# Cross attention of a fused decoder: more copies in flight early, every fifth key-block maximum copied by ScalarE, five pairs ahead of the loop instead of twelve

## The chip, the core and the metric

The kernel runs as one program on one core of a Trainium2 chip. The metric is the device time of one execution in microseconds (us); smaller is better.

## The reference

The program is a decoder of two layers on 1024 tokens of width 128, with a context of 6404 keys. Only the first cross attention concerns us here:

```
q = (x @ Wq + bq).reshape(1, 1024, 8, 16)      # 8 heads of 16
k = (ctx @ Wk + bk).reshape(1, 6404, 8, 16)
v = (ctx @ Wv + bv).reshape(1, 6404, 8, 16)
weight = softmax(einsum('bhqd,bhkd->bhqk', q, k) / 4)
out = einsum('bhqk,bhkd->bhqd', weight, v) @ Wo + bo
x = x + out
```

Before it stands a fast-weight attention, behind it a mixture of experts, a Mamba layer, a second cross attention and a second mixture. The change touches none of those.

## The kernel before

The stage is `xattn0_stage`. Its work is cut into four units: unit `u` is half of the tokens (512) for one group of four heads. Keys lie in SBUF as bf16 parts, features on the partitions. Softmax takes two passes over the keys. The first finds, for each query and head, the maximum score, from an approximate product of 64 rows. The second computes scores with the negative maximum as extra key and query rows, takes the exponential and weighs the values.

**First pass.** A pair is two heads of 128 queries against 496 keys: two matmuls side by side into two PSUM banks (`maximum`). A unit has 104 pairs, numbered so that four groups of 128 queries (`qt` 0 to 3) are innermost, then two head pairs (`h`), then 13 key blocks. VectorE reduces each bank (`take`, L1253). The ring for this is three banks, M0 to M2; entry `e` of the ring uses banks `2e % 3` and `(2e + 1) % 3`, so TensorE may fill entry `e` once the first bank of entry `e - 1` is free (`free_banks`, L1145).

**Early part.** The maxima of unit 0 come ahead of everything. Of each four pairs, three go into psE, are copied by ScalarE to `copied` in bf16 (L1101) and merged by VectorE into six running maxima (`merge`, L1266 and L1268). The fourth goes through the ring. There are 26 such groups of four. Then `end_running` folds the running maxima (L1275, L1278) and `give_maxima` turns 16 columns into three bf16 parts. TensorE transposes them (L1178), ScalarE copies them (L1083), and three transfers on SyncE's queue place them as rows of `qs` (L1055). The scores of unit 0 wait for these rows (`m_placed`).

**Lead.** Behind that, `LEAD` pairs of unit 1 go through the ring (one ahead of the transposition, the rest behind it) before TensorE comes to the first scores. Each has to have its banks freed by VectorE.

**Loop.** A unit has 51 tiles of 128 keys. For tile `t` TensorE issues, in this order: the scores of tile `t + 1` (two halves of two matmuls, L1158), then a pair of the next unit's first pass (call it *a*), then the weighing of tile `t` (`weigh`, L1171, eight records), then another pair (*c*). Some tiles have three pairs: the extra one stands between the halves of the scores, so the order is half, *a*, half, *b*, weigh, *c*. ScalarE takes the two exponentials of a tile (L1112); VectorE takes the pairs in turn. Once in a unit *c* is replaced by the transposition of the next unit's maxima (`PLACE_AT`), by the sums (L1183) and by the output projection (L1189). VectorE also inverts the sums in four pieces after the pairs of tiles 4, 8, 10 and 12 (L1316). The last pair of a unit is followed by `give_maxima` on VectorE.

SyncE issues the loads in program order on one queue: near keys (four blocks), queries of units 1 to 3, more constants, and then the far keys (heads 4 to 7, needed from unit 2 on), seven transfers of 832 KB and one of ones, also 832 KB. All that is issued by 420 us of the span. Behind it stand the rows of the maxima and the loads of the values.

Of the kernel before, what the change touches and what calls it, by code (L numbers as in the profile page):

```python
# [16 lines left out]
P = 128  # L17
# [5 lines left out]
BF16 = mybir.dt.bfloat16  # L23
# [3 lines left out]
ALU = mybir.AluOpType  # L27
ACT = mybir.ActivationFunctionType
# [920 lines left out]
def xattn0_stage(nc, k, d):  # L949
# [5 lines left out]
    with ExitStack() as ctx:  # L955
# [11 lines left out]
            .rearrange("p (i j n) -> p i j n", i=6, j=2)  # L967
        copied = sb("copied", [P, 2, 2, CHUNK0], BF16)
        maxima = sb("maxima", [P, 4, 4, CHUNKS0 + 1])
# [7 lines left out]
        psO = ps("O", [P, 512])  # L977
        psM = [ps(f"M{i}", [P, 512]) for i in range(3)]

# [6 lines left out]
        scored, exped, pv = sem("scored"), sem("exped"), sem("pv")  # L986
        max_mm, max_done = sem("max_mm"), sem("max_done")
        m_ready, m_tr, m_row, m_placed = sem("m_ready"), sem("m_tr"), sem("m_row"), sem("m_placed")
        o_copied, s_mm, s_copied, inverted, on_done, y_mm, y_done = [
            sem(n) for n in ("o_copied", "s_mm", "s_copied", "inverted", "on_done", "y_mm", "y_done")]  # L990
        LOADS = 2
        UNITS = 4
        PAIRS = 8 * CHUNKS0
        EARLY = PAIRS // 4
        LEAD = 12
        PLACE_AT, SUMS_AT, OUTPUT_AT = 46, 2, 20
        INVERT_AT = (4, 8, 10, 12)

        def kinds_in_tile(u, t):

            if u == UNITS - 1:
                return {SUMS_AT: ["sums"], OUTPUT_AT: ["output"]}.get(t, [])
            kinds = ["max"] * (3 if t in ((12, 24, 36) if u == 0 else (6, 14, 28, 36, 41)) else 2)
            if t == PLACE_AT:
                kinds[-1] = "place"
            if u and t == SUMS_AT:
                kinds[-1] = "sums"
            if u and t == OUTPUT_AT:
                kinds[-1] = "output"
            return kinds  # L1010
# [12 lines left out]
        def pair_place(pair):  # L1023

            return pair // 8, pair // 4 % 2, pair % 4

        with nc.Block() as block:
# [50 lines left out]
            def _(e):  # L1078
# [18 lines left out]
                for n in range(3 * EARLY):  # L1097
                    e.wait_ge(pre_mm, 2 * n + 2)
                    if n >= 2:
                        e.wait_ge(pre_merged, n - 1)  # L1100
                    nc.scalar.activation(copied[:, n % 2, :, :], psE[:, 2 * (n % 2):2 * (n % 2) + 2, 0:CHUNK0],  # L1101
                                         ACT.Copy).then_inc(pre_copied, 1)
                put_maxima_in_rows(0, EARLY + 1)

                def weights(u, t, g):
# [24 lines left out]
            def _(e):  # L1130
# [12 lines left out]
                def free_banks(entry):  # L1143

                    e.wait_ge(max_done, max(2 * entry - 1, 0))  # L1145
                    return psM[2 * entry % 3], psM[(2 * entry + 1) % 3]

                def next_maximum(u, pair, entry):
                    if (u, pair) == (2, 0):
                        e.wait_ge(far_keys_in, 16 * (len(K_ROWS) + 1))  # L1150
                    maximum(u, pair, [bank[:, 0:CHUNK0] for bank in free_banks(entry)], max_mm)

# [90 lines left out]
            def _(e):  # L1243
# [4 lines left out]
                def take(u, pair, entry):  # L1248
# [6 lines left out]
                    if pair == PAIRS - 1:  # L1255
                        e.wait_ge(max_done, 2 * entry + 2)
                        give_maxima(u)

                def merge(n, pair):
# [5 lines left out]
                    if n < 6:  # L1265
                        V.tensor_copy(mine, copied[:, n % 2, :, :]).then_inc(pre_merged, 1)  # L1266
                    else:
                        V.tensor_tensor(mine, mine, copied[:, n % 2, :, :], ALU.max).then_inc(pre_merged, 1)  # L1268

# [12 lines left out]
                def give_maxima(u):  # L1282
                    if u == 0:
                        end_running()
                    columns = maxima[:, :, :, 0:CHUNKS0 + (u == 0)]
                    step(V.tensor_reduce(mneg[:], columns.rearrange("p j q n -> p (j q) n"), AX.X, ALU.max, negate=True))
                    step(V.tensor_copy(mpart[:, 0, :], mneg[:]))
# [9 lines left out]
                def pass_on(semaphore, count, entry):  # L1297

                    e.wait_ge(semaphore, count)
                    if entry:  # L1300
                        e.wait_ge(max_done, 2 * entry)
                    e.sem_inc(max_done, 2)
# [25 lines left out]
                for u in range(UNITS):  # L1328
                    for t in range(TILES0):
                        for kind, entry, pair_unit, pair in in_tile.get((u, t), ()):  # L1330
                            if kind == "max":
                                take(pair_unit, pair, entry)
# [1614 lines left out]
```

## Time and profile before

| | us |
|---|---|
| median of 3 runs | 2831.26 (2829.81 to 2834.96) |
| profiled execution, its own time | 2832.58 |
| its span | 2830.8 |
| first pair of the early part starts | 386.1 |
| last reduction of the early part starts | 478.03 |
| first scores of the loop start | 501.09 |
| output of unit 0 copied | 640.36 |
| output of unit 3 copied | 1031.59 |
| stage over (last addition to x starts) | 1041.14 |

The span runs from the first to the last instruction; the execution's own time is 1.8 us more. Busy shares over the whole span are averages over six stages. In the table the stage lies between 386 and 1042 us. "Idle before" names the time for which an engine did nothing ahead of an instruction, and what ended it.

### The profile page before, as it was taken

How to read it: one execution, taken by the hardware profiler on the slowest of the kernel's cores; microseconds unless marked ns; L12 is line 12 of the kernel's file. 1: busy time of each engine (PE TensorE's matmuls, PEld its weight loads, DVE VectorE, ACT ScalarE, POOL GpSimd, SP SyncE). 2: the span in 40 equal slices, each digit the busy share in tenths (PEclk: the TensorE clock that was granted, in tenths of full speed). 3: DMA queues.
4: the chain of work that ended last, by engine and by line, in shares of the span. 5: the costliest groups of instructions: out<-in, count | busy, mean ns of one | idle time of the engine just before them, and what ended most of it. 6: DMA issues, size and time to landing. Idle time of an engine off the chain costs nothing. (4 is left out here: it accounts for less than half of the span.)

```text
span 2830.8 us, 35253 instructions
## 1 busy us (share of the span) xinstructions
PE 2419.0 (85%) x10344; PEld 891.7 (31%) x10344; DVE 2091.2 (74%) x3087; ACT 1538.3 (54%) x1858; POOL 297.4 (11%) x330
## 2 busy tenths in 40 slices
PE   5888735999999978999566589999999999995997
PEld 3655400222222123444222223333333333332443
DVE  5666648999998024444597889999999999966665
ACT  5544546676767962333343566666666666652111
POOL 4655600000000000000054000000000000000000
PEclk8998955999999989999688589999999999997998
DMA  4333399000000106766000521112003010112000
GB/s 115 131 125 122 130 150 113 21 24 25 24 25 25 32 27 180 191 191 182 24 0 12 116 78 45 30 55 77 29 29 103 29 30 29 32 35 103 0 0 7
DMA packets 186252, 190.66 MB, mean 67 GB/s; under 512 B 18464, under 2 KB 158181, under 8 KB 184801
## 3 DMA queue, kind: packets, MB, share of 16 engines
q1 hardware_dynamic: 186125, 189.00, 25.9%
q8 instruction: 75, 1.23, 0.2%
q14 instruction: 52, 0.43, 0.1%
HBM read 144.05 MB, written 41.42 MB: 66 GB/s over the span
## 5 line engine op out<-in xcount | busy, mean ns | idle before, releaser
L2468 DVE TENSOR_TENSOR y_acc<-y_acc,y_probs 128x1024 f32<-128x1024 f32 x408 | 496.2, 1216 | 33.8 <-ACT y_probs L2164 23.5
L2164 ACT ACTIVATE y_probs<-y_E,y_mask_bias 128x1024 f32<-128x1024 f32 x416 | 440.8, 1111 | 66.1 <-PE y_E L2249 66.0
L1112 ACT ACTIVATE x_probs<-x_E 128x1024 f32<-128x1024 f32 x408 | 396.8, 1021 | 137.0 <-PE x_E L1158 134.6
L1253 DVE TENSOR_REDUCE x_maxima<-x_M 128x1 f32<-128x496 f32 x676 | 420.1, 667 | 25.7 <-PE x_M L1140 14.0
L2258 PE MATMUL y_O<-y_probs,y_values 128*64 128x512 f32 x1664 | 402.3, 604 | 0.0
L2248 PE MATMUL y_E<-y_qa,y_ks 128*128 128x512 f16 x832 | 319.2, 384 | 1.2 <-ACT y_copied L2140 1.2
L2249 PE MATMUL y_E<-y_qb,y_ks 66*128 66x512 f16 x832 | 317.5, 382 | 0.0
L2140 ACT ACTIVATE y_copied<-y_M 128x1024 bf16<-128x1024 f32 x164 | 167.8, 1023 | 210.0 <-PE y_M L2215 210.0
L2406 DVE TENSOR_REDUCE y_maxima<-y_M 128x2 f32<-128x1024 f32 (+1 forms) x195 | 238.5, 1223 | 35.6 <-PE y_M L2215 23.5
L1577 DVE TENSOR_TENSOR f_hidden<-f_act_out,f_spread 128x512 f32<-128x512 f32 x160 | 110.6, 692 | 169.5 <-ACT f_act_out L1461 162.0
L1158 PE MATMUL x_E<-qs,x_keys 128*128 128x512 bf16 x816 | 220.2, 384 | 4.8 <-ACT x_probs L1112 2.9
L1171 PE MATMUL x_O<-x_probs,x_values 128*32 128x512 f32 x1632 | 217.3, 605 | 0.6 <-ACT x_probs L1112 0.6
L1461 ACT ACTIVATE f_act_out<-f_b 128x512 f32<-128x512 f32 x160 | 95.4, 597 | 185.0 <-PE f_b L1493 185.0
L2215 PE MATMUL y_M<-y_ks,y_qa 64*128 64x512 f16 x742 | 148.6, 397 | 26.8 <-DVE y_maxima L2406 24.1
L1498 PE MATMUL f_b<-f_hidden,f_weights 128*128 128x512 f32 x320 | 164.1, 596 | 4.9 <-DVE f_hidden L1577 4.9
L1493 PE MATMUL f_b<-f_xnT,f_weights 128*128 128x512 f32 x320 | 165.1, 598 | 1.1 <-ACT f_act_out L1461 1.1
L1140 PE MATMUL x_M<-x_keys,qs 64*128 64x496 bf16 x338 | 136.5, 404 | 23.8 <-DVE x_maxima L1253 23.3
L2258 PEld LDWEIGHTS y_O<-y_probs,y_values 128*64 128x64 f32 x1664 | 101.5, 136 | 171.1 <-issue 164.0
L2674 PE MATMUL g_b<-g_w_in,g_xT 128*128 128x512 f32 x256 | 120.0, 611 | 23.5 <-ACT g_xT L2634 17.0
L1140 PE MATMUL x_M<-x_keys,qm 64*128 64x496 bf16 x338 | 136.6, 404 | 0.0
L2417 DVE TENSOR_TENSOR y_running<-y_running,y_copied 128x1024 bf16<-128x1024 bf16 x192 | 131.1, 683 | 3.7 <-ACT y_copied L2140 3.4
L2248 PEld LDWEIGHTS y_E<-y_qa,y_ks 128*128 128x128 f16 x832 | 81.5, 98 | 141.5 <-issue 45.5
(460 smaller groups left out, 3035.7 us busy)
## 6 DMA issues: line engine op xcount, KB each, us to landing
f_spread<-comb_dram SPq DMA_DIRECT2D x160, 256.0 KB, 3.9
y_values<-v_dram SPq DMA_DIRECT2D x208, 128.0 KB, 2.2
v_dram<-a_v_out SPq DMA_DIRECT2D x26, 512.0 KB, 2.7
k_dram<-a_k_parts SPq DMA_DIRECT2D x26, 512.0 KB, 3.3
x_values<-v_dram SPq DMA_DIRECT2D x100, 128.0 KB, 2.1
f_weights<-f_w_in SPq DMA_DIRECT2D x80, 128.0 KB, 2.3
y_ks<-k_dram SPq DMA_DIRECT2D x75, 128.0 KB, 2.7
v_dram<-a_v_out SPq DMA_DIRECT2D x26, 256.0 KB, 2.0
```

What stands on the lines that cost most here:

```text
L1112: nc.scalar.activation(probs[:, n % 2, 2 * g:2 * g + 2, :], psE[:, 2 * g:2 * g + 2, :], ACT.Exp).then_inc(exped, 1)
L1140: T.matmul(banks[j], q, ks[r, 4 * (u // 2) + 2 * h + j, CHUNK0 * c:CHUNK0 * c + CHUNK0], start=True, stop=True).then_inc(done, 1)
L1158: ins = T.matmul(psE[:, j, :], ks[:, 4 * (u // 2) + j, P * t:P * t + P], qs[:, u, j, :], start=True, stop=True)
L1171: ins = T.matmul(psO[32 * j:32 * j + 32, :], values[:, i, 32 * j:32 * j + 32], probs[:, n % 2, j, :], start=(t == 0), stop=(t == TILES0 - ...
L1253: V.tensor_reduce(maxima[:, 2 * h + j, qt, c:c + 1], psM[(2 * entry + j) % 3][:, 0:CHUNK0], AX.X, ALU.max).then_inc(max_done, 1)
L2140: A(out, scores, ACT.Copy).then_inc(S["spare_copied"], 1)
L2164: A(probs[:, i, :], psE[:, 2 * (i % 2):2 * (i % 2) + 2, :].rearrange("p a b -> p (a b)"), ACT.Exp, bias=mask_bias[:, bass.ds(c * TILES_IN_ ...
L2248: T.matmul(psE[:, 2 * slot + j, :], ks1[:, u // 2 % 2, keys], qa[:, u, j, :], start=True, stop=False)
L2249: ins = T.matmul(psE[:, 2 * slot + j, :], ks2[:, u // 2 % 2, keys], qb[:, u, j, :], start=False, stop=True)
L2258: ins = T.matmul(psO[u % 2][DH1 * j:DH1 * j + DH1, :], values[:, i, DH1 * j:DH1 * j + DH1], probs[:, i, 512 * j:512 * j + 512], start=Fals ...
L2406: V.tensor_reduce(maxima[:, u % 2, :, 2 * g, bass.ds(c, 1)], psO_pair[:] if (u, g) == (0, 1) else psM[:], AX.X, ALU.max)\
L2468: ins = V.tensor_tensor(acc[:, u % 2, :], acc[:, u % 2, :], probs[:, i, :], ALU.add)
```

## The change

Four edits are made in `xattn0_stage`:

1. `copied` has four slots instead of two: in the early part, ScalarE's copy `n` waits for merge `n - 4` instead of `n - 2`.
2. In the loop, some *c* pairs (those with `qt` 2 or 3, at most every second tile, not the last eight pairs of a unit) are "spare": TensorE announces them on another semaphore, ScalarE copies both banks to bf16 after the second exponential of the next tile (`copy_spare`), in one instruction where the banks are neighbours, else in two. The first copy of each of four slots in a unit goes straight to `spares`; the others go to `copied` and are merged by VectorE two tiles later, ahead of its pairs (`merge_spare`). VectorE's reductions of these pairs are gone. The entry after a spare one needs ScalarE's whole copy. `give_maxima` first folds the four slots (`end_spares`) and afterwards resets `maxima`. By the selection loop 61 pairs of the loop are spare (21, 21 and 19 in the loops of units 0, 1 and 2), 20 of them copied in two pieces; 49 have a merge. (The loops hold 110, 104 and 93 pairs.)
3. `LEAD` is 5 instead of 12, and unit 0 has nine tiles of three pairs instead of three (110 pairs instead of 104; unit 2 has 93 instead of 92).
4. `PLACE_AT` is 47 instead of 46.

```diff
-        copied = sb("copied", [P, 2, 2, CHUNK0], BF16)
+        copied = sb("copied", [P, 4, 2, CHUNK0], BF16)
+        spares = sb("spares", [P, 4, 2, CHUNK0], BF16)
...
-        LEAD = 12
-        PLACE_AT, SUMS_AT, OUTPUT_AT = 46, 2, 20
+        LEAD = 5
+        PLACE_AT, SUMS_AT, OUTPUT_AT = 47, 2, 20
...
-            kinds = ["max"] * (3 if t in ((12, 24, 36) if u == 0 else (6, 14, 28, 36, 41)) else 2)
+            kinds = ["max"] * (3 if t in ((3, 8, 13, 18, 23, 28, 33, 38, 42) if u == 0 else (6, 14, 28, 36, 41)) else 2)
...
+        for u in range(UNITS - 1):
+            for t in range(TILES0 - 1):
+                kind, entry, unit, pair = in_tile.get((u, t), [("none", 0, 0, 0)])[-1]
+                _, h, qt = pair_place(pair)
+                if kind != "max" or qt < 2 or pair >= PAIRS - 8 or TILES0 * u + t < turn + 2:
+                    continue
+                slot, turn = 2 * h + qt - 2, TILES0 * u + t
+                new = (unit, slot) not in seen
+                seen.add((unit, slot))
+                spare[unit, pair] = len(spare), slot, None if new else merges
+                merges += not new
+                by_act.add(entry)
+                merge_at.setdefault(((turn + 2) // TILES0, (turn + 2) % TILES0), []).append((unit, pair))
...
                 for n in range(3 * EARLY):
                     e.wait_ge(pre_mm, 2 * n + 2)
-                    if n >= 2:
-                        e.wait_ge(pre_merged, n - 1)
+                    if n >= 4:
+                        e.wait_ge(pre_merged, n - 3)
...
+                def copy_spare(unit, pair, entry):
+                    n, slot, m = spare[unit, pair]
+                    e.wait_ge(spare_mm, 2 * n + 2)
+                    if m is None:
+                        if unit >= 2:
+                            e.wait_ge(m_ready, unit)
+                        out = spares[:, slot, :, :]
+                    else:
+                        if m >= 4:
+                            e.wait_ge(spare_merged, m - 3)
+                        out = copied[:, m % 4, :, :]
+                    bank = 2 * entry % 3
+                    if bank < 2:
+                        ins = nc.scalar.activation(out, psM3[:, bank:bank + 2, 0:CHUNK0], ACT.Copy)
+                    else:
+                        for j in range(2):
+                            ins = nc.scalar.activation(out[:, j, :], psM[(bank + j) % 3][:, 0:CHUNK0], ACT.Copy)
+                    ins.then_inc(spare_copied, 1)
...
                         weights(u, t, 1)
-                        for kind, entry, _, _ in in_tile.get((u, t - 1), ()):
+                        for kind, entry, pair_unit, pair in in_tile.get((u, t - 1), ()):
+                            if kind == "max" and (pair_unit, pair) in spare:
+                                copy_spare(pair_unit, pair, entry)
...
                 def free_banks(entry):
-                    e.wait_ge(max_done, max(2 * entry - 1, 0))
+                    if entry:
+                        e.wait_ge(max_done, vector_banks[entry - 1] + (entry - 1 not in by_act))
+                    if scalar_pairs[entry]:
+                        e.wait_ge(spare_copied, scalar_pairs[entry])
...
+                def end_spares(u):
+                    last = [found for (unit, _), found in spare.items() if unit <= u]
+                    e.wait_ge(spare_copied, len(last))
+                    e.wait_ge(spare_merged, sum(m is not None for _, _, m in last))
+                    width = CHUNK0
+                    while width > 62:
+                        width //= 2
+                        step(V.tensor_tensor(spares[:, :, :, 0:width], spares[:, :, :, 0:width],
+                                             spares[:, :, :, width:2 * width], ALU.max))
+                    for h in range(2):
+                        ins = V.tensor_reduce(maxima[:, 2 * h:2 * h + 2, 2:4, CHUNKS0].rearrange("p j q -> p q j"),
+                                              spares[:, 2 * h:2 * h + 2, :, 0:width], AX.X, ALU.max)
+                    step(ins)
...
                     if u == 0:
                         end_running()
+                    else:
+                        end_spares(u)
...
+                    if u + 1 < UNITS:
+                        step(V.memset(maxima[:], LOWEST))
...
                     for t in range(TILES0):
+                        for pair_unit, pair in merge_at.get((u, t), ()):
+                            merge_spare(pair_unit, pair)
```

`merge_spare` waits for the copy and the merge before, and issues one `V.tensor_tensor(mine, mine, copied[...], ALU.max)` on 128x992 bf16, the same form as L1268.

## Rows read from the trace of the kernel before

**Rows 1.** Windows of units 0 and 3: us busy (count) by engine, clock, DMA.
```profile
501.00:640.00 139.00, 135.82 (x825) 33.91 (x823) 130.80 (x216) 100.47 (x104) 0.00 (x0) 0.99 0.09 24
...
922.00:1031.00 109.00, 105.69 (x626) 21.02 (x618) 4.07 (x5) 98.79 (x103) 1.27 (x1) 1.00 0.11 31
```

**Rows 2.** Timeline of TensorE, one two-pair tile: start, length, instruction.
```profile
705.10 0.38 PE L1140 MATMUL x_M<-x_keys,qs 64*128 64x496 bf16 x1
...
706.41 0.38 PE L1140 MATMUL x_M<-x_keys,qs 64*128 64x496 bf16 x1
...
706.73 1.04 PE L1158 MATMUL x_E<-qs,x_keys 128*128 128x512 bf16 x4
...
707.70 0.38 PE L1140 MATMUL x_M<-x_keys,qs 64*128 64x496 bf16 x1
```

**Rows 3.** Reductions of one pair, in that tile's timeline, and their group.
```profile
L1253 DVE TENSOR_REDUCE x_maxima<-x_M x676: 608/665/676, 389.9 to 910.6; 128x1 f32<-128x496 f32 x169
...
705.52 1.25 DVE L1253 TENSOR_REDUCE x_maxima<-x_M 128x1 f32<-128x496 f32 x2
```

**Rows 4.** Timeline of TensorE around a tile of three pairs (unit 1, tile 6).
```profile
657.91 0.38 PE L1140 MATMUL x_M<-x_keys,qs 64*128 64x496 bf16 x1 [0.45 <-DVE x_maxima L1253]
...
659.06 0.38 PE L1140 MATMUL x_M<-x_keys,qs 64*128 64x496 bf16 x1 [0.23 <-DVE x_maxima L1253]
...
661.54 0.38 PE L1140 MATMUL x_M<-x_keys,qs 64*128 64x496 bf16 x1
```

**Rows 5.** The reciprocal ahead of that stall, in the timeline.
```profile
656.38 0.94 DVE L1316 RECIPROCAL x_recip<-x_sums 128x128 f32<-128x128 f32 x1
```

**Rows 6.** Timeline of ScalarE: two exponentials of a steady tile.
```profile
707.37 1.94 ACT L1112 ACTIVATE x_probs<-x_E 128x1024 f32<-128x1024 f32 x2 [0.66 <-PE x_E L1158]
```

**Rows 7.** ScalarE's early copies (timeline), and its copy of one bank.
```profile
398.43 2.79 ACT L1101 ACTIVATE x_copied<-x_E 128x992 bf16<-128x992 f32 x3 [0.75 <-PE x_E L1140]
...
L1089 ACT ACTIVATE x_o_sb<-x_O x4: 597/597/597, 640.4 to 1031.6; 128x512 f32<-128x512 f32 x4
```

**Rows 8.** VectorE's merges in one early group, timeline.
```profile
401.22 1.25 DVE L1268 TENSOR_TENSOR x_probs<-x_probs,x_copied 128x992 bf16<-128x992 bf16 x2
403.00 0.68 DVE L1268 TENSOR_TENSOR x_probs<-x_probs,x_copied 128x992 bf16<-128x992 bf16 x1 [0.54 <-ACT x_copied L1101]
```

**Rows 9.** TensorE's timeline, last lead pairs and first scores.
```profile
499.20 0.59 PE L1140 MATMUL x_M<-x_keys,qs 64*128 64x496 bf16 x1 [0.77 <-DVE x_maxima L1253]
...
500.56 0.59 PE L1140 MATMUL x_M<-x_keys,qs 64*128 64x496 bf16 x1 [0.76 <-DVE x_maxima L1253]
...
501.09 1.89 PE L1158 MATMUL x_E<-qs,x_keys 128*128 128x512 bf16 x4
...
504.69 0.38 PE L1140 MATMUL x_M<-x_keys,qs 64*128 64x496 bf16 x1
```

**Rows 10.** DMA issues from 375 to 500 us: size, median us to landing.
```profile
x_keys<-key_ones_in SPq DMA_DIRECT2D x1, 832.0 KB, 72.3
...
qs<-x_mrow SPq DMA_DIRECT2D x3, 4.0 KB, 3.7
```

**Rows 11.** Window with a low DMA share (last but one).
```profile
488.00:488.50 0.50, 0.18 (x2) 0.10 (x2) 0.50 (x2) 0.12 (x1) 0.00 (x0) 0.50 0.06 3
```

**Rows 12.** Timeline: VectorE's folding of the early maxima.
```profile
479.31 3.26 DVE L1275 TENSOR_TENSOR x_probs<-x_probs 128x2976 bf16<-128x2976 bf16 x3
482.60 0.99 DVE L1278 TENSOR_REDUCE x_maxima<-x_probs 128x6 f32<-128x372 bf16 x2
```

**Rows 13.** TensorE held by give_maxima in unit 0, timeline.
```profile
626.13 0.38 PE L1140 MATMUL x_M<-x_keys,qs 64*128 64x496 bf16 x1 [1.45 <-DVE x_maxima L1253]
```

**Rows 14.** Windows: granted clock behind the sums of unit 3, and at the first scores.
```profile
1036.00:1038.00 2.00, 0.00 (x0) 0.00 (x0) 1.63 (x3) 0.00 (x0) 0.29 (x1) 0.56 0.00 0
...
503.00:504.00 1.00, 0.76 (x2) 0.13 (x2) 0.00 (x0) 1.00 (x2) 0.00 (x0) 0.61 0.00 0
```

**Rows 15.** Timeline: the sums of unit 3.
```profile
1032.24 1.12 PE L1183 MATMUL x_M<-x_o_sb,x_sum_rows 128*128 128x512 f32 x2 [0.72 <-ACT x_o_sb L1089]
```

More of the change, by code:

```diff
@@ L977, in xattn0_stage @@
         psO = ps("O", [P, 512])
-        psM = [ps(f"M{i}", [P, 512]) for i in range(3)]
+        psM3 = ps("M", [P, 3, 512])
+        psM = [psM3[:, i, :] for i in range(3)]
         keys_in, far_keys_in = [sem(f"keys_in{b}") for b in range(4)], sem("far_keys_in")
@@ L987, in xattn0_stage @@
         max_mm, max_done = sem("max_mm"), sem("max_done")
+        spare_mm, spare_copied, spare_merged = sem("spare_mm"), sem("spare_copied"), sem("spare_merged")
         m_ready, m_tr, m_row, m_placed = sem("m_ready"), sem("m_tr"), sem("m_row"), sem("m_placed")
@@ L1025, in pair_place @@
             return pair // 8, pair // 4 % 2, pair % 4
+        spare, merge_at, by_act = {}, {}, set()
+        seen, merges, turn = set(), 0, -2
+        for u in range(UNITS - 1):
[11 more added lines that the diff above has]
+                merge_at.setdefault(((turn + 2) // TILES0, (turn + 2) % TILES0), []).append((unit, pair))
+        vector_banks = [2 * sum(e not in by_act for e in range(n)) for n in range(LAST_ENTRY + 3)]
+        scalar_pairs = [sum(e in by_act for e in range(n)) for n in range(LAST_ENTRY + 3)]
         with nc.Block() as block:
@@ L1098, in _ @@
                     e.wait_ge(pre_mm, 2 * n + 2)
-                    if n >= 2:
-                        e.wait_ge(pre_merged, n - 1)
-                    nc.scalar.activation(copied[:, n % 2, :, :], psE[:, 2 * (n % 2):2 * (n % 2) + 2, 0:CHUNK0],
+                    if n >= 4:
+                        e.wait_ge(pre_merged, n - 3)
+                    nc.scalar.activation(copied[:, n % 4, :, :], psE[:, 2 * (n % 2):2 * (n % 2) + 2, 0:CHUNK0],
                                          ACT.Copy).then_inc(pre_copied, 1)
@@ L1150, in next_maximum @@
                         e.wait_ge(far_keys_in, 16 * (len(K_ROWS) + 1))
-                    maximum(u, pair, [bank[:, 0:CHUNK0] for bank in free_banks(entry)], max_mm)
+                    maximum(u, pair, [bank[:, 0:CHUNK0] for bank in free_banks(entry)],
+                            spare_mm if (u, pair) in spare else max_mm)
                 def scores(u, t, g):
@@ L1255, in take @@
                     if pair == PAIRS - 1:
-                        e.wait_ge(max_done, 2 * entry + 2)
+                        e.wait_ge(max_done, vector_banks[entry] + 2)
                         give_maxima(u)
@@ L1265, in merge, with merge_spare @@
                     if n < 6:
-                        V.tensor_copy(mine, copied[:, n % 2, :, :]).then_inc(pre_merged, 1)
+                        V.tensor_copy(mine, copied[:, n % 4, :, :]).then_inc(pre_merged, 1)
                     else:
-                        V.tensor_tensor(mine, mine, copied[:, n % 2, :, :], ALU.max).then_inc(pre_merged, 1)
+                        V.tensor_tensor(mine, mine, copied[:, n % 4, :, :], ALU.max).then_inc(pre_merged, 1)
+                def merge_spare(unit, pair):
+                    n, slot, m = spare[unit, pair]
+                    if m is None:
+                        return
+                    e.wait_ge(spare_copied, n + 1)
+                    if m:
+                        e.wait_ge(spare_merged, m)
+                    mine = spares[:, slot, :, :]
+                    V.tensor_tensor(mine, mine, copied[:, m % 4, :, :], ALU.max).then_inc(spare_merged, 1)
+                def end_spares(u):
[11 more added lines that the diff above has]
+                    step(ins)
                 def end_running():
@@ L1284, in give_maxima @@
                         end_running()
-                    columns = maxima[:, :, :, 0:CHUNKS0 + (u == 0)]
-                    step(V.tensor_reduce(mneg[:], columns.rearrange("p j q n -> p (j q) n"), AX.X, ALU.max, negate=True))
+                    else:
+                        end_spares(u)
+                    step(V.tensor_reduce(mneg[:], maxima[:].rearrange("p j q n -> p (j q) n"), AX.X, ALU.max, negate=True))
+                    if u + 1 < UNITS:
+                        step(V.memset(maxima[:], LOWEST))
                     step(V.tensor_copy(mpart[:, 0, :], mneg[:]))
@@ L1300, in pass_on @@
                     if entry:
-                        e.wait_ge(max_done, 2 * entry)
+                        e.wait_ge(max_done, vector_banks[entry])
                     e.sem_inc(max_done, 2)
@@ L1329, in _ @@
                     for t in range(TILES0):
+                        for pair_unit, pair in merge_at.get((u, t), ()):
+                            merge_spare(pair_unit, pair)
                         for kind, entry, pair_unit, pair in in_tile.get((u, t), ()):
+                            if kind == "max" and (pair_unit, pair) in spare:
+                                continue
                             if kind == "max":
```

## The prediction

> **What bounds the kernel now.** I read the slices of the page first: all of the change lies in one stage, from 386 to 1042 us. Then I read windows by unit. In unit 0 TensorE is busy for 135.8 of 139 us at full clock, VectorE for 130.8, ScalarE for 100.5 [rows 1]. Two engines look full, and busy shares can't say which is the bound, so I read one tile in the timeline. The reader is to see that TensorE's starts leave nothing over: *a* to *c* 1.31 us (a pair and the weighing), *c* to scores 0.32, scores to the next *a* 0.97, in all 2.60 us a tile [rows 2], with no idle note on any of them. Taking a pair away from a tile would save some 0.31 us; having VectorE do less would save nothing.
>
> VectorE's records hide slack. Two reductions take 1.25 us of which one is 0.665, so the second starts 0.585 after the first [rows 3]. The first starts 0.42 after its matmul (705.10 to 705.52). VectorE is thus ready for the next pair 0.42 + 1.17 = 1.59 us after the matmul started, and that pair's reduction is wanted at 1.29 + 0.42 = 1.71: 0.12 us to spare. The bank for the next matmul is free at 0.42 + 0.665 + 0.06 = 1.15 us, wanted at 1.29: 0.14 us to spare. TensorE is the bound in two-pair tiles and VectorE follows closely, so any delay above about 0.26 us on VectorE is felt.
>
> It is felt in three places. In a three-pair tile the pairs follow at 1.15 us, not at the 0.8 that half the scores need; from the last pair of the tile before to the last of this one it takes 661.54 - 657.91 = 3.63 us, 1.04 more than a two-pair tile (2.59 to 2.60) [rows 4]. A reciprocal (0.86 us of VectorE's turn) leaves TensorE idle for 0.45 [rows 4, 5]. give_maxima leaves it idle for 1.45 [rows 13]. ScalarE waits 0.66 us in each tile for scores [rows 6]. In unit 3, with no pairs, a tile takes 109 / 51 = 2.14 us [rows 1].
>
> **Ahead of the loop.** In the early part ScalarE's third copy is late by one merge, which costs VectorE 0.54 us of idle time in a group [rows 8]; four slots take that away, 26 x 0.54 = 14 us. ScalarE's three copies need 2.79 us [rows 7], less than VectorE's five operations at about 0.59 (2.95), so nothing else steps in. The lead pairs are 1.36 us apart [rows 9]; seven fewer give 9.5 us. Together 23.5 us, if the loop could start then. It can't: it waits for the rows of the maxima, and these are transfers behind the far keys on one queue. The last of the far keys, issued at 419 us (see the order of issues), landed 72.3 us later, at 491.3; the rows issued from 486.85 on took 3.7 us although they are 4 KB each [rows 10]. The share of DMA fell only at 488 [rows 11]. No engine's work pulls that time forward. The rows would be issued near 473 now, and land when the backlog is gone, between 488 and 491.5. I take 490: the loop starts 501.1 - 490 = **11.1 us earlier** (9.6 to 13). Shortening the lead alone would give nearly all of it (501.1 - 9.5 = 491.6), so the 14 us of the early part are worth about 1.6.
>
> The Trainium skill (DMA: Bandwidth & Descriptors, section on queues, rings and completion order) says that each DMA engine takes the descriptors of one ring in order, while completion as a whole isn't in order of issue. The trace agrees with the first half: small transfers behind large ones land late, by the rows above. By the second half a small transfer on engines that drain early could land sooner; that is a rival below.
>
> **Moved pairs.** Seven pairs go from the lead into loops: six make three-pair tiles in unit 0 at 1.04 each [rows 4], one is an ordinary pair in unit 2 (0.31). **+6.5 us** (bounds 7 x 0.31 = 2.2, were VectorE no hindrance, and 7.3).
>
> **Waiting for ScalarE's copy.** A spare *c* started at, say, 706.41 is finished 0.38 later. ScalarE has just ended its second exponential (0.66 of idle time are next), so its copy starts at 0.42. It is a 128x992 copy; three take 2.79, and at about 0.9 between starts one takes 1.0 [rows 7]. Two halves take about 0.6 each, the second starting some 0.5 behind: 1.07. The next *a* needs the whole copy: 0.42 + 1.0 + 0.06 = 1.48 us after *c*, or 1.55, where it was wanted at 1.29. TensorE waits 0.19 us 41 times and 0.26 us 20 times: 13.0. VectorE would have freed a bank at 1.15, in time; so the copy is a new wait, on a shorter way. Before a three-pair tile (12 of them follow a spare *c*) the wait was there already, at 1.15, and becomes 1.48: 0.14 more than counted, 1.7. **+14.7 us** (bounds: 3, if a copy costs 0.05; 20, at 0.33 each).
>
> The exponentials are delayed by 0.42 + 0.9 - 0.96 = 0.36 us (0.43 in halves; scores are done at 0.32 + 0.64 = 0.96). TensorE needs the second one only for the second half of the scores of the next tile, 0.45 us after it ends now (707.37 - 0.66 = 706.71 against 706.73 + 0.43 = 707.16) [rows 2, 6]. So this is covered, barely; were it not, each spare pair would cost 0.36 to 0.43 instead of 0.19 to 0.26.
>
> **Merges.** A merge takes 0.585 us of VectorE's turn (1.25 - 0.665) [rows 8]. It stands right ahead of the reductions of *a*, two tiles after the copy. The hole that the missing reductions left was one tile earlier and is no use to it. By the reciprocal, 0.86 us gave a stall of 0.45 (the idle note; records overlap by up to 0.07, so 0.52) [rows 4, 5]: 0.34 to 0.41 is swallowed. With 0.34, estimated on the dear side, a merge costs 0.25; 49 of them 12.3. Where VectorE has no slack the full time counts: six fall into three-pair tiles by the selection (13, 28, 33 and 42 in unit 0, tile 6 in units 1 and 2), four follow a reciprocal (tiles 11 and 13 in units 1 and 2): 10 x 0.33 = 3.3. Two reciprocals, in tile 4 of units 1 and 2, stand where a spare pair is skipped and get hidden: -0.5 each. **+14.6 us** (bounds 8 at 0.17 each; 26 at the naive delay of 0.47).
>
> **Folding.** give_maxima now begins with end_spares: three maxima over 1984, 992 and 496 results. The early one had 2976, 1488 and 744 in 3.26 us [rows 12]; with 0.665 for 992 this is 0.13 fixed and 0.535 per thousand, so 2.35 us. Two reductions of 248 elements against two of 372 in 0.99 [rows 12]: 0.75. The memset of 224 elements has no row in this stage; I take 0.2, between nothing and 0.5 (one of those reductions). Sum 3.3 us, in which VectorE frees no bank. TensorE was idle already for 1.45 [rows 13], so all of it is felt in the loops of units 0 and 1. In unit 2 no pair follows; the transposition at tile 47 comes some 6.5 us after the last pair and would wait about 0.5. **+7.1 us** (6 to 8).
>
> **Clock.** TensorE would thus be idle for 1.45 + 3.3 = 4.75 us twice. After the sums of unit 3 it ended at 1033.4 [rows 15], and in the window from 1036 the granted clock is 0.56, so it fell from 2.4 to 1.2 GHz at about 1036.2, after 2.8 us without work [rows 14]. It should fall here too. At the loop's start, at 1.2 GHz, two rounds of scores and a start of *a* took 3.6 us for what is 2.3 at full clock [rows 2, 9]; the clock rose near 503.8 [rows 14]. **+2.6 us** for two falls (0 to 4).
>
> The Trainium skill (TensorE: Matmul & The Clock Gate, section on HAM oscillation) says that idle gaps between bursts of matmuls can throttle the clock anew each time. By it the sum keeps this term; with the clock held it would be 2863 us.
>
> **The sum.** -11.1 + 6.5 + 14.7 + 14.6 + 7.1 + 2.6 = **+34.4 us** against the profiled execution's own 2832.58, 1.3 above the median of 2831.26. From the median: **2866 us**. The bounds of the terms, not all on one side, give 2842 to 2884.
>
> **Rivals.**
> - *VectorE is the bound (faster).* Busy for 131 of 139 us [rows 1], it may hold TensorE all along in ways that no idle note shows. Then 12 spare pairs save 1.17 each and 49 save 0.585, 42.7 us, as far as TensorE allows. TensorE's own need in a unit is 51 x 1.97 (a tile without its two pairs) + 104 x 0.31 + about 2 = 135, against 139 in unit 0 and (922 - 640) / 2 = 141 in units 1 and 2: 18 us to gain at most. With -11.1, +2.2 for the pairs and +7.1 for the folding it gives -20: 2811. It decides if *a* comes within 1.29 us of a spare *c*. The idle notes in three-pair tiles speak for it, the evenness of rows 2 against. 0.10.
> - *ScalarE falls behind.* The exponentials' cover of 0.45 us isn't enough: 41 x 0.36 + 20 x 0.43 = 23.4 instead of 13.0. 2876. For it: 1.94 + 0.9 is more than a tile's 2.60 [rows 2, 6, 7]. Against: at most every second tile. 0.14.
> - *The rows overtake the far keys.* The loop starts when the lead is done, 23.5 us earlier instead of 11.1: 2854. Against: 3.7 us for 4 KB [rows 10]. 0.11.
> - *The new waits are nearly nothing* (0.05 for a copy, 0.17 for a merge, no fall of the clock): 2866 - 11 - 7 - 3 = 2845. 0.08.
>
> **The numbers.** My forecast has 0.54; 0.03 are left for a plain draw. Within 0.2% (5.7 us) is about what a measurement of this kernel can't tell from no change. Faster 0.12, same 0.06, slower 0.82. The range of 8 in 10 leaves out the faster rival and some of the tails: 2838 to 2882.
>
> **What would show it.** The first scores near 490 (near 478 if the rows overtake), after an idle wait that ends with the transfer to `qs`; early groups of about 2.95 us; *a* 1.48 us after a spare *c*, with ScalarE as releaser; *a* to *c* 1.5 to 1.6 in tiles with a merge; two idle times of about 4.8 us in units 0 and 1, and a clock below 1 behind them; units of 150 us or more. If unit 1 takes less than 138 us, TensorE wasn't the bound and I am wrong. If *a* follows a spare *c* in 1.3 us, the third term falls.

## The result and the profile after

The changed kernel takes 2883.06 us (median of 4, 2882.01 to 2887.2) where the kernel before took 2832.11 us beside it (2829.81 to 2834.96): a ratio of 1.0182, 95% interval 1.0164 to 1.0200, or 51 us more. The forecast was 2866 us, slower, with a range from 2838 to 2882. The direction was right; the size was two thirds of the real one, and the time lies 1 us above the range.

In the kernel after, L1101 has become L1122, L1158 is L1205, L1171 is L1218, the pairs (L1140) are L1183, their reductions (L1253) L1300, the early merges (L1268) L1315, the merges in the loop L1325, and ScalarE's copies of spare pairs L1150 (in one piece) and L1153 (in two).

First the way to the loop: timelines of VectorE, TensorE and SyncE of the kernel after, between 457 and 502 us.

```profile
457.43 1.25 DVE L1300 TENSOR_REDUCE x_maxima<-x_M 128x1 f32<-128x496 f32 x2
458.59 1.83 DVE L1315 TENSOR_TENSOR x_probs<-x_probs,x_copied 128x992 bf16<-128x992 bf16 x3
460.35 1.25 DVE L1300 TENSOR_REDUCE x_maxima<-x_M 128x1 f32<-128x496 f32 x2
...
476.64 0.59 PE L1183 MATMUL x_M<-x_keys,qs 64*128 64x496 bf16 x1 [0.77 <-DVE x_maxima L1300]
...
496.68 1.49 PE L1205 MATMUL x_E<-qs,x_keys 128*128 128x512 bf16 x3 [19.44 <-DMA qs<-x_mrow]
...
472.45 2.18 SPq L1076 DMA_DIRECT2D qs<-x_mrow  x3
```

An early group now takes 460.35 - 457.43 = 2.92 us, its three merges without a gap ([rows 8] had 0.54 us of idle time ahead of the third). The lead is done at 477. Then TensorE is idle for 19.4 us, and what ends that is a transfer. The same stretch in the view of DMA issues, and one window (DMA share last but one):

```profile
x_keys<-key_ones_in SPq DMA_DIRECT2D x1, 832.0 KB, 76.0
...
qs<-x_mrow SPq DMA_DIRECT2D x3, 4.0 KB, 22.2
...
490.00:492.00 2.00, 0.00 (x0) 0.00 (x0) 0.00 (x0) 0.00 (x0) 0.00 (x0) 0.50 0.99 107
```

Rows of 4 KB took 22.2 us to land where they took 3.7 in [rows 10]; the last transfer of the far keys, issued at 419.6, landed 76.0 later, at 495.6, and the queue is still full at 490 to 492. The loop starts at 496.7, 4.4 us earlier than the 501.1 of [rows 9].

Then the loop. Timeline of TensorE, ScalarE and VectorE of the kernel after, in unit 1 (tile 15, which has a merge ahead of *a* and a spare *c*, and the start of tile 16):

```profile
710.53 0.38 PE L1183 MATMUL x_M<-x_keys,qs 64*128 64x496 bf16 x1
...
712.14 0.38 PE L1183 MATMUL x_M<-x_keys,qs 64*128 64x496 bf16 x1 [0.23 <-DVE x_maxima L1300]
...
713.73 0.37 PE L1183 MATMUL x_M<-x_keys,qs 64*128 64x496 bf16 x1 [0.24 <-ACT x_copied L1150]
...
712.59 1.00 ACT L1150 ACTIVATE x_copied<-x_M 128x992 bf16<-128x992 f32 x1 [0.45 <-PE x_M L1183]
...
710.83 0.67 DVE L1325 TENSOR_TENSOR x_spares<-x_spares,x_copied 128x992 bf16<-128x992 bf16 x1
711.41 1.25 DVE L1300 TENSOR_REDUCE x_maxima<-x_M 128x1 f32<-128x496 f32 x2
```

The reader is to see two stretched steps. From *a* (710.53) to the spare *c* (712.14) it is 1.61 us instead of 1.31, since a merge stands ahead of the reductions of *a*. From that *c* to the next *a* (713.73) it is 1.59 instead of 1.29 [rows 2], since ScalarE's copy begins 0.45 after *c*, lasts 1.00, and TensorE starts another 0.14 behind its end. Both new waits are on TensorE's way.

Third, the folding: timelines of the kernel after at the end of unit 0, and windows with the granted clock (third from the right).

```profile
639.51 2.35 DVE L1334 TENSOR_TENSOR x_spares<-x_spares 128x1984 bf16<-128x1984 bf16 x3
641.90 0.73 DVE L1337 TENSOR_REDUCE x_maxima<-x_spares 128x4 f32<-128x248 bf16 x2
...
643.16 0.24 DVE L1360 MEMSET x_maxima<- 128x224 f32 x1
...
645.45 0.59 PE L1183 MATMUL x_M<-x_keys,qs 64*128 64x496 bf16 x1 [4.98 <-DVE x_maxima L1300]
...
644.00:648.00 4.00, 2.55 (x8) 0.64 (x8) 3.09 (x8) 0.95 (x2) 0.00 (x0) 0.58 0.02 4
...
651.00:652.00 1.00, 1.00 (x4) 0.25 (x2) 0.00 (x0) 1.00 (x2) 0.00 (x0) 0.78 0.00 0
```

TensorE's idle time is 4.98 us where [rows 13] have 1.45, and the clock behind it is 1.2 GHz until about 651.4. The end of unit 1 shows the same: 4.98 us of idle time until 806.89, and 1.2 GHz until about 811.9.

The waits of TensorE in the kernel after, from 497 us to the end of the stage (total, times, longest), show the new class:

```profile
PE x_M L1183 <- DVE x_maxima L1300: 32.5, 69, 5.0
PE x_E L1205 <- DMA qs<-x_mrow: 19.4, 1, 19.4
PE x_M L1183 <- ACT x_copied L1150: 11.1, 32, 0.7
PE x_M L1183 <- ACT x_copied L1153: 6.4, 17, 0.7
...
PE x_M L1183 <- ACT x_spares L1150: 1.9, 8, 0.2
...
PE x_M L1183 <- ACT x_spares L1153: 1.3, 3, 0.7
```

In the kernel before the first of these was 13.4 us, 37 times, and the others didn't exist. The four lines that end with ACT are 60 waits for ScalarE's copies, 20.7 us in all. VectorE's busy time over the whole span fell (2091.2 to 2049.2 us) and the kernel got slower.

### The profile page after: what moved, and what is told of

It reads as the page before. It is cut to its first block and busy times, and to the rows that moved or that the text cites. A ratio compares the mean times of both kernels' runs of the same rounds, so it can differ in the third digit from the quotient of the medians.

```text
span 2880.2 us, 35626 instructions
## 1 busy us (share of the span) xinstructions
PE 2422.9 (84%) x10286; PEld 893.7 (31%) x10344; DVE 2049.2 (71%) x3032; ACT 1594.4 (55%) x1939; POOL 298.2 (10%) x330
## 5 line engine op out<-in xcount | busy, mean ns | idle before, releaser
L1300 DVE TENSOR_REDUCE x_maxima<-x_M 128x1 f32<-128x496 f32 x554 | 344.6, 668 | 130.8 <-PE x_M L1183 125.3
L1205 PE MATMUL x_E<-qs,x_keys 128*128 128x512 bf16 x758 | 213.2, 387 | 31.1 <-DMA qs<-x_mrow 19.4
L1218 PE MATMUL x_O<-x_probs,x_values 128*32 128x512 f32 x1632 | 219.3, 609 | 0.7 <-ACT x_probs L1133 0.6
L1183 PE MATMUL x_M<-x_keys,qs 64*128 64x496 bf16 x338 | 135.4, 401 | 62.9 <-DVE x_maxima L1300 41.3
L1183 PE MATMUL x_M<-x_keys,qm 64*128 64x496 bf16 x338 | 136.3, 403 | 0.0
```

What stands on the lines that cost most here:

```text
L1183: T.matmul(banks[j], q, ks[r, 4 * (u // 2) + 2 * h + j, CHUNK0 * c:CHUNK0 * c + CHUNK0], start=True, stop=True).then_inc(done, 1)
L1205: ins = T.matmul(psE[:, j, :], ks[:, 4 * (u // 2) + j, P * t:P * t + P], qs[:, u, j, :], start=True, stop=True)
L1218: ins = T.matmul(psO[32 * j:32 * j + 32, :], values[:, i, 32 * j:32 * j + 32], probs[:, n % 2, j, :], start=(t == 0), stop=(t == TILES0 - ...
L1300: V.tensor_reduce(maxima[:, 2 * h + j, qt, c:c + 1], psM[(2 * entry + j) % 3][:, 0:CHUNK0], AX.X, ALU.max).then_inc(max_done, 1)
```

## The experiments

The length of a unit turned out a sharp measure: from the first scores (or the copy of the output of the unit before) to the copy of its own output, by starts in the timeline. Unit 3 takes 108.9 us in every kernel for which I read the units. The table holds these lengths; the last two columns are the start of the loop and the median of all runs. The kernel before took 2832.3, 2832.3 and 2831.5 us beside the three groups of runs. I write "before" and "after" for the two kernels.

| run | unit 0 | unit 1 | unit 2 | loop | start | median |
|---|---|---|---|---|---|---|
| before | 139.3 | 143.3 | 139.0 | 530.5 | 501.1 | 2832.1 |
| after | 164.7 | 161.4 | 151.0 | 586.0 | 496.7 | 2883.1 |
| e1, no spare pairs | 145.8 | 143.3 | 139.2 | 537.3 | 492.9 | 2832.8 |
| e2, four slots only | 138.9 | 143.3 | 139.0 | 530.1 | 494.3 | 2823.2 |
| e3, short lead only | 146.4 | 143.3 | 139.3 | 538.0 | 494.6 | 2831.0 |
| e4, spare pairs unread | 146.1 | 143.4 | 137.5 | 535.9 | 491.3 | 2829.4 |
| e5, no merges | 158.6 | 156.0 | 145.5 | 569.0 | 498.6 | 2866.6 |
| e6, copies only | 154.0 | 150.1 | 145.5 | 558.5 | 494.8 | 2851.6 |
| e7, folding spread | 162.1 | 159.8 | 153.6 | 584.5 | 492.9 | 2877.4 |

**e1: the spare pairs taken out.**

```diff
-                if kind != "max" or qt < 2 or pair >= PAIRS - 8 or TILES0 * u + t < turn + 2:
+                if True:
                     continue
```

with the folding and the reset of `maxima` gone too.

> The changed kernel with no spare pairs: VectorE reduces all of them, no merges, no folding, no memset; four slots, a lead of five and nine three-pair tiles stay. Theory (TensorE is the bound in the loop; each spare pair adds waits): the loop loses only the moved pairs, 6 to 7 us over the kernel before, and starts 4 to 10 us earlier; total within -4 to +3 us of the kernel before, about 2832, 50 us below the changed kernel. Rival (VectorE is the bound and spare pairs relieve it): slower than the changed kernel or equal to it, 2880 or more.

Measured 2832.79 us (2826.95 to 2837.86, 10 runs), ratio to before 1.0004 (0.9995 to 1.0014). The spare pairs with all that belongs to them cost 50 us, and the other three edits together (slots, lead with the moved pairs, `PLACE_AT`) come to nothing: the start is earlier, unit 0 is 6.5 us longer, units 1 and 2 are as before. The rival that VectorE is the bound has fallen.

**e2: four slots alone.** The early part of the change on the kernel before (`copied` with four slots, `n >= 4`, `n - 3`).

> The kernel before with four slots for the early copies and nothing else. Early groups 2.92 us instead of 3.54, so the last lead pair is done near 487. Theory (the rows of the maxima land only when the far keys have landed): the first scores start when the rows land, between 490 and 496.5 and not at 487, a gain of 5 to 10 us: 2822 to 2827. Rival (the rows don't wait for the far keys): 487, a gain of 14 us, 2818.

Measured 2823.16 us, ratio 0.9963 (0.9950 to 0.9976): faster. TensorE's timeline in this run, the last lead pair and the first scores:

```profile
488.25 0.59 PE L1140 MATMUL x_M<-x_keys,qs 64*128 64x496 bf16 x1 [0.77 <-DVE x_maxima L1253]
...
494.28 1.48 PE L1158 MATMUL x_E<-qs,x_keys 128*128 128x512 bf16 x3 [5.43 <-DMA qs<-x_mrow]
```

The lead is done, and TensorE waits 5.4 us more for the rows. So of the 12.3 us by which the lead is done earlier (488.25 against 500.56), 6.8 arrive in this execution; by the medians the gain is 9.2.

**e3: the short lead alone.**

```diff
-        LEAD = 12
+        LEAD = 5
...
-            kinds = ["max"] * (3 if t in ((12, 24, 36) if u == 0 else (6, 14, 28, 36, 41)) else 2)
+            kinds = ["max"] * (3 if t in ((3, 8, 13, 18, 23, 28, 33, 38, 42) if u == 0 else (6, 14, 28, 36, 41)) else 2)
```

> The kernel before with a lead of five pairs and the nine three-pair tiles, two slots as before. Rows are issued at 487 as before. Theory: first scores at 491.5, 9.5 us earlier, and 6.2 us lost to six more three-pair tiles at 1.04 us each plus 0.3 for one pair more: 2829, 3 us faster. Rival (a pair costs TensorE only its own 0.31 us): 2825. On the far keys: if faster early copying slows their transfer, they end at 491 here, as before, and 4 to 5 us later in the two kernels with four slots; if their end only varies by itself, no such order shows.

Measured 2831.01 us, ratio 0.9996 (0.9986 to 1.0006): no change. The start was 494.6, not 491.5, since here too the last far keys landed late (issued 419.9, landed 73.6 later, 493.5). Unit 0 is 7.1 us longer (6.5 in e1 with the same tiles) and unit 2 0.3. What the lead gives, the three-pair tiles take. (Unit 0 is 0.6 us longer here than in e1, which has `PLACE_AT` at 47 and this run at 46; no run changes `PLACE_AT` alone.) This run has two slots, so the late end of the far keys doesn't come from faster copying. Over the nine kernels of the table, one profiled execution each, that end (issue and landing of the last transfer) ranges from 490.1 (e4) to 497.8 us (e5), in no order that follows the edits.

**e4: relief without its price.** The 61 spare pairs are computed, and no engine reads them (their part of the maxima is missing). TensorE waits for its own matmuls before it writes a bank again.

```diff
-                    if scalar_pairs[entry]:
-                        e.wait_ge(spare_copied, scalar_pairs[entry])
+                    if scalar_pairs[entry]:
+                        e.wait_ge(spare_mm, 2 * scalar_pairs[entry])
```

> The changed kernel in which the 61 spare pairs are computed but read by nobody (ScalarE's copies, the merges and the folding are left out, so that part of the maxima is missing): the relief of VectorE without its price. Theory (TensorE is the bound): 5 to 7 us below the run without spare pairs, from three-pair tiles behind a spare pair and two hidden reciprocals. Rival (VectorE is the bound): about 18 us below it, 2815 or less.

Measured 2829.42 us, 3.4 below e1 by the medians; by the loops 1.4 (535.9 against 537.3), in unit 2 1.7. Were the copies free, taking 61 pairs off VectorE would give about this: less than my 5 to 7 and far from 18. (`maxima` is still reset here, one instruction of 0.245 us in units 0 and 1, so the relief itself is up to 0.5 us more.)

**e5: no merges.** `merge_spare` isn't called, so what it would take in is missing from the maxima; copies and folding stay.

> The changed kernel without its 49 merges in the loop (the copies that a merge would take in are left out of the maxima); copies, folding and the rest stay. Theory (VectorE follows TensorE closely, each merge is felt by 0.25 to 0.30 us, some in full): 13 to 18 us below the changed kernel, 2865 to 2870. Rival (merges run in the hole that the missing reductions leave): within 3 us of the changed kernel.

Measured 2866.63 us, 16.4 below the changed kernel. By the loops the 49 merges cost 17.0 us (6.1, 5.4 and 5.5 in units 0 to 2).

**e6: copies only.** As e5, and `end_spares` and the `memset` are gone too (all of the spare pairs' part is missing).

> The changed kernel with ScalarE's 61 copies, but no merges, no folding and no reset of the maxima (their part of the maxima is left out). What stays over the run without spare pairs is the wait of TensorE for ScalarE's copies, less the small relief that the run with unread pairs showed. Theory: 0.30 us for a copy in one piece and 0.37 in two, some more ahead of three-pair tiles, 20 us, less 3: 2847 to 2855, and 15 to 20 us below the run without merges, of which folding is 7 and the clock 6. Rival (the waits were mis-sized and the folding and its clock are most): below 2842.

Measured 2851.59 us: 18.8 above e1 by the medians and 21.2 by the loops (8.2, 6.8, 6.3). That is the price of the copies, VectorE's relief already taken off. The trace of e6 shows where it comes from: from a spare *c* to the next *a* it is 1.59 us at all 41 copies in one piece and 1.65 at all 20 in two, instead of 1.29 (1.15 ahead of a three-pair tile). Against e5 it is 15.0 by the medians, but e5 happened to start 3.8 us later; by the loops folding, reset and clock cost 10.5 (4.6, 5.9 and 0 in unit 2, where no pair follows). TensorE's idle time in `give_maxima` is 4.98 us in e5 and 1.47 in e6, in both units, so 3.5 of each is the longer idle time; what is left, 1.1 in unit 0 and 2.4 in unit 1, is what the low clock behind it costs, an estimate.

**e7: the folding spread.** The three maxima stand ahead of tile 43, within it and ahead of tile 44, with the two reductions; nothing is left out.

```diff
+                        if u < UNITS - 1 and t == 43:
+                            fold_spares(u + 1, 248)
+                        if u < UNITS - 1 and t == 44:
+                            fold_spares(u + 1, 62)
+                            end_spares(u + 1)
+                        for i, (kind, entry, pair_unit, pair) in enumerate(in_tile.get((u, t), ())):
+                            if u < UNITS - 1 and t == 43 and i == 1:
+                                fold_spares(u + 1, 124)
```

> The changed kernel with the folding spread: its three maxima and two reductions stand in tiles 43 and 44 between pairs, ahead of the last pair of the unit, and no longer in give_maxima. All work is still done. Theory: the idle time of TensorE in give_maxima falls from 5.0 to about 1.8 us, the clock stays at 2.4 GHz (twice 2.9 us), and each piece is partly swallowed: 7 to 10 us below the changed kernel, 2873 to 2876. Rival (the clock's fall costs nothing that matters): 1 to 3 us below it.

Measured 2877.37 us, 5.7 below the changed kernel. In the profiled executions the start is 3.8 us earlier, and the loop is shorter by 1.5 only. Here I was wrong. TensorE's timeline of this run at the end of unit 0:

```profile
632.68 0.38 PE L1183 MATMUL x_M<-x_keys,qs 64*128 64x496 bf16 x1 [0.88 <-DVE x_maxima L1300]
...
634.56 0.38 PE L1183 MATMUL x_M<-x_keys,qs 64*128 64x496 bf16 x1 [0.52 <-DVE x_maxima L1300]
...
636.93 0.38 PE L1183 MATMUL x_M<-x_keys,qs 64*128 64x496 bf16 x1 [1.00 <-DVE x_maxima L1300]
...
641.43 0.38 PE L1183 MATMUL x_M<-x_keys,qs 64*128 64x496 bf16 x1 [1.84 <-DVE x_maxima L1300]
```

and its clock (third from the right) in windows around them, and in two windows at the end of unit 1:

```profile
636.00:640.00 4.00, 2.66 (x16) 0.66 (x16) 3.71 (x10) 1.94 (x2) 0.00 (x0) 1.00 0.00 0
640.00:644.00 4.00, 2.56 (x16) 0.66 (x16) 3.85 (x10) 1.61 (x2) 0.00 (x0) 1.00 0.13 37
...
801.00:802.00 1.00, 1.00 (x8) 0.30 (x10) 0.98 (x3) 1.00 (x2) 0.00 (x0) 0.76 0.00 0
...
804.00:805.00 1.00, 1.00 (x5) 0.40 (x4) 0.00 (x0) 0.90 (x2) 0.00 (x0) 0.53 0.00 0
```

In unit 0 the last idle time is 1.84 us and the clock stays up, as expected. In unit 1 the idle times are the same to 0.01 us, but there the clock is low from about 801.5 to 804.9, so the expectation failed in that unit. And the pieces aren't swallowed: 0.88 + 0.52 + 1.00 + 1.84 = 4.24 us against 4.98. The rest of the gain in unit 0, 2.6 - 0.7 = 1.9, is what the fall of the clock had cost there, an estimate. In unit 1 the same difference is 1.6 - 0.7 = 0.9, with 3.4 us of low clock left instead of 6.8. Unit 2, which had hidden the folding, loses 2.6. With the estimates of e6 a fall costs 1.1 to 2.4 us here.

**e8 and e9: the far keys out of the way.** Instead of one block of eight transfers ahead of the rows, the far keys are issued in 32 pieces of at most 248 KB, one behind each load of values; TensorE waits for a block of them per 32 pairs of unit 2.

```diff
-                load_keys(far, slice(0, KVP), far_keys_in)
...
                         sp.dma_start(values[:, i:i + n, :], d.v0_dram[:, t:t + n, P * hg:P * hg + P])\
                             .then_inc(v_loaded[g % 2], 16)
+                        load_far_piece()
```

e8 has this on e2:

> The kernel before with four slots for the early copies, and the far keys issued in 32 pieces of at most 248 KB, one behind each load of values from the start of the loop on, instead of all at once ahead of the rows. Theory (the rows wait for the far keys): rows land 2 to 4 us after their issue at 473, the loop starts when the lead is done, at 487, a gain of 14 us: 2818, and 4 to 7 us below the kernel with four slots alone. Rival (the rows are slow for another reason, or the pieces hold up the loads of values and with them the weighing): start at 490 or later, or stalls on the values; 2824 or more.

and e9 on the changed kernel:

> The changed kernel with the far keys issued in pieces behind the loads of values, so that the rows of the maxima have nothing ahead of them; all work is done. The lead is done near 478. Theory (in the changed kernel the loop's start at 496.7 is set by the far keys alone, and the rest of its loss lies in the loop): the loop starts near 478, 18 to 19 us earlier: 2864 to 2866, still 32 us above the kernel before. Rival (part of the loop's loss comes from the late start or the full queue): below 2860.

e8: 2818.92 us, ratio 0.9953 (0.9936 to 0.9970). e9: 2864.89 us, ratio 1.0117 (1.0101 to 1.0134). The view of DMA issues of e8, and TensorE's timeline there at the last lead pair and the first scores:

```profile
qs<-x_mrow SPq DMA_DIRECT2D x3, 4.0 KB, 1.7
...
488.34 0.59 PE L1154 MATMUL x_M<-x_keys,qs 64*128 64x496 bf16 x1 [0.76 <-DVE x_maxima L1267]
...
488.87 1.89 PE L1172 MATMUL x_E<-qs,x_keys 128*128 128x512 bf16 x4
```

With nothing ahead of them the same rows land in 1.7 us, and the scores start right behind the lead. The loop then lasts 531.4 us, 1.2 longer than in e2. In e9 the loop starts at 477.3 and lasts 585.8 us, as long as in the changed kernel: start and loop don't mix, and the changed kernel's loss lies in the loop.

**e10 and e11: a version that beats both.** On e8, the near keys go ahead of the queries of units 1 to 3, and their first block is cut in four, so that the first pair needs 496 keys only.

```diff
+NEAR_BLOCKS = [slice(496 * b, 496 * b + 496) for b in range(4)] + KEY_BLOCKS[1:]
...
-                for b in range(2):
-                    load_keys(near, KEY_BLOCKS[b], keys_in[b])
+                for b in range(7):
+                    load_keys(near, NEAR_BLOCKS[b], keys_in[b])
```

> Kernel before, four slots, far keys in pieces, and near keys ahead of the queries of units 1 to 3 and of the constants, the first block of near keys in four blocks of 496 keys. Lead of twelve as before, no spare pairs. TensorE waited for its first keys until 386 (issued at 367). Theory: the first pair starts near 373, the early part is held by VectorE at 2.93 us a group, and all that follows moves up: 11 to 14 us below the run with far keys in pieces, 2805 to 2808. Rival (small transfers are slower, or a later block comes late and gives the time back): above 2812.

> The same with a lead of five pairs and nine three-pair tiles. Theory: with nothing in the way of the rows the shorter lead gives its 9.5 us (or what the rows leave of it, they need some 4 us from the transposition on) and costs 6.5 in the loop: 2 to 3 us below the run with the long lead. Rival: no difference or slower, if the clock, low for longer, takes the rest.

e10: 2812.25 us, ratio 0.9936 (0.9919 to 0.9953), 4 above my figure. e11: 2809.15 us, ratio 0.9920 (0.9903 to 0.9937). Their intervals overlap, so the lead stays undecided (in the profiled executions e11 starts its loop 8.3 us earlier, at 471.3, and takes 7.0 longer for it). TensorE's timeline and waits in e10:

```profile
373.99 0.57 PE L1153 MATMUL x_E<-x_keys,qs 64*128 64x496 bf16 x1 [14.03 <-DMA x_keys<-key_ones_in]
...
PE x_E L1153 <- DMA x_keys<-key_ones_in: 20.5, 2, 14.0
```

The first pair starts 12 us earlier. A second wait of 20.5 - 14.0 = 6.5 us for a later block gives part of it back, as the rival had it: the loop starts at 479.6, 9.3 earlier than in e8.

## Why the prediction was right in sign and short in size

The mechanisms were the forecast ones, all five of them. What failed are the sizes of two terms: the earlier start, forecast as 11.1 us and measured as 4.4, and the wait for ScalarE's copies, forecast as 14.7 and measured as 21.2. They are 13.2 of the 16.7 us between the two sums.

The five terms of the sum and what the runs gave for each (loops against e1, e6, e5 and before; the start from the profiled executions):

| term | predicted | measured |
|---|---|---|
| earlier start of the loop | -11.1 | -4.4 |
| moved pairs | +6.5 | +6.8 |
| wait for ScalarE's copies | +14.7 | +21.2 |
| merges | +14.6 | +17.0 |
| folding, reset, clock | +9.7 | +10.5 |
| sum | +34.4 | +51.1 |

- **TensorE is the bound, VectorE isn't: right.** e1 and e4 bear it out; the faster rival was wrong. VectorE's 131 busy of 139 us was real work, and 61 pairs less of it are worth 1.4 us, or some 2 with the reset of e4 taken off.
- **The start (the first term): right mechanism, mis-sized by 6.7 us.** The rows did wait for the far keys; the rival that they overtake is refuted by the 19.4 us of idle time and by e8. What failed is the step "land when the backlog is gone, between 488 and 491.5": I took the end of the far keys of one execution as fixed. It was 491.3 there and 495.6 in the kernel after. In the eight profiled kernels where the rows came last (after, e1 to e7) the loop started between 491.3 and 498.6 us, 494.5 on average. So the fair value is 6.6 us, and single executions give 2.5 to 9.8. Worked out from the medians and the lengths of the loops instead (an estimate, as only profiled executions show their loops), the same kernels gain 4.2 to 8.9 us, 7.3 on average: 11.1 was too much for each of them. Why the same bytes end at different times stays open; e3, with the slow early copying, shows that faster copying isn't needed for it. The kernel before hid this spread under its long lead. By the rule that each DMA engine takes a ring's descriptors in order (the Trainium skill, DMA: Bandwidth & Descriptors, queues, rings and completion order) rows behind such a backlog would wait for it; the trace agrees, with 22.2 against 1.7 us.
- **Moved pairs: right.** 1.04 us for a pair in a three-pair tile, by rows of one such tile, gave 6.5; measured 6.8 in e1 and 7.5 in e3.
- **Waiting for the copy (the third term): right mechanism, mis-sized by 6.5 us.** I had *c* to *a* at 1.48 us; it is 1.59. For a copy in two pieces it is 1.65 where I had 1.55. The copy starts 0.45 after *c*, not 0.42, and TensorE starts 0.14 to 0.15 behind its end (712.59 + 1.00 against 713.73), not 0.06. The 0.06 was VectorE's, carried over to ScalarE, where no row showed a wait of TensorE on a copy of these banks. With these two numbers the prediction's own sum comes out as measured: 41 x 0.30 + 20 x 0.36 + 1.7 = 21.2. The second rival (exponentials late) didn't come: TensorE's waits on exponentials are 3.5 us in the kernel before and in e6, which has all the copies, and 5.8 in the kernel after.
- **Merges: nearly right.** A merge costs 0.30 us (1.61 against 1.31), not 0.25. 49 x 0.05 is the miss of 2.4. That they don't run in the hole left by the reductions is shown by e5.
- **Folding and clock: right.** An idle time of 4.98 us was forecast as 4.75; the clock fell as forecast, at an estimated 1.1 to 2.4 us where I had 1.3. The 0.5 us forecast for unit 2 didn't come. What e7 disproved is my later guess that spreading the folding would win 7 us or more: a piece of 1.2 us between two pairs still costs 0.9.
- **The range** ended 1 us too low. It treated the terms as independent, and its upper bound left no room for a start without its gain beside a dear copy. The two errors are alike: a latency and a landing time were read off a single row each.

## What to carry to other kernels

When two engines are both nearly full, compare start-to-start times of the critical engine in one tile with its own work before relieving the other; here a ring of three banks made each release part of TensorE's way, and a consumer that frees banks later than the old one costs even if it has idle time to spare. Work inserted on the engine that follows closely is felt beyond its slack of about 0.3 us, and each insertion pays anew. A small transfer that gates a loop should not be issued behind a bulk load on its queue, however early the bulk load was issued: moving the bulk behind it brought the gain of the four slots from 9 to 13 us, and nothing tried in the loop gave as much.

## What the runs showed of the hardware

- TensorE resumed 0.14 to 0.15 us after the end of ScalarE's copy of two PSUM banks (712.59 + 1.00 to 713.73; at 60 of the 61 copies of the kernel after), but 0.06 us after the end of VectorE's reduction of one (all 37 waits of the kernel before and 69 of the kernel after).
- The same far keys behind the same near keys ended between 490.1 and 497.8 us in different profiled kernels.
- With TensorE idle for 4.98 us the granted clock fell to 1.2 GHz and stayed there until about 651.4, 6 us after TensorE had resumed; at the start of the loop after 19.4 us of idle time it rose some 4.6 us after TensorE resumed (0.87 on average from 501 to 502). The cost of a fall in mid-loop is estimated at 1.1 to 2.4 us from e5, e6 and e7; the clock was low for 4 to 6 us of TensorE's work, and no run shows why the cost is less than half of that.
- In e7, the same four idle times (4.24 us in all, the longest 1.84) left the clock at 2.4 GHz in unit 0 and were followed by 3.4 us at 1.2 GHz in unit 1, beginning at about 801.5, 1.5 us after TensorE had resumed.
